# Two adaLN blocks, experts of the second: every expert on every row, or each row in blocks of its two experts

## Chip, cores and metric

One Trainium2 chip, one core. The metric is the device time of one launch in microseconds (us), the median of the runs shown. The engines are called TensorE (PE in the rows, PEld for its weight loads), VectorE (DVE), ScalarE (ACT), GpSimd (POOL) and SyncE (SP). SP, ACT and POOL can issue transfers by DMA.

## What is computed

Two transformer blocks with modulation from a condition, on 32 sequences of 256 rows of 128 numbers, all float32. Block 0 has attention with one head and a feed-forward part whose inputs are quantised to FP4 in groups of 16. Block 1 has causal attention with 16 heads and a mixture of 4 usable experts (8 are given, 4 reserved), of which each row takes the two with the largest weight:

```
logits = xf @ gate_w.T
logits = where(expert_ids >= E - N_RESERVED, -inf, logits)
top_w, top_idx = top_k(softmax(logits), 2)
top_w = top_w / sum(top_w)
cw = zeros((T, E)).at[arange(T)[:, None], top_idx].add(top_w)
h = silu(einsum('td,edh->teh', xf, w1)) * einsum('td,edh->teh', xf, w3)
y = einsum('teh,ehd->ted', h, w2)
out = einsum('te,ted->td', cw, y)
...
x = x + gb * out
```

d is 128, h is 704 (five chunks of 128 and a tail of 64). Routing depends on the data.

## The kernel before

**Pairs and turns.** Two sequences (512 rows, four tiles of 128) make a pair; there are 16. The program is a software pipeline: one turn of it holds work on up to five pairs. `sp_order`, `pool_order`, `act_order`, `dve_order` and `pe_order` (L98 to L163) are lists written out by a planner: `do(3, "turn2")` means the step turn2 on the pair that is three ahead of the turn's own. `turns` (L440) runs a list for the turns -4 to 15; turns 1 to 11 are a hardware loop. Each engine goes through its list in order, and a step waits on semaphores for what it reads. Leads 4 and 3 are block 0 (normalise, attention, quantise, feed forward), leads 3 to 1 block 1's attention and routing, leads 1 and 0 the experts. `USES` (L71) says which of seven PSUM banks a step uses, in the order in which the banks pass from one to the next; the eighth bank is `y_ps`.

**The experts before.** All weights stay in SBUF: `wg_hi`, `wg_lo`, `wu_hi`, `wu_lo` (each a float32r half of the gate or up weights) and `wd`. The 4 x 704 columns are 22 chunks. For each chunk `gate` (L1517) and `up` (L1525) call `product` (L1488): three float32r matmuls of 128 x 128 weights with all 512 rows of the pair (high with high, low with high, high with low). ACT takes tanh of the gate bank (L828), DVE makes two passes of 512 elements (`swish` L1197, `times` L1205), and `down` (L1501) adds the chunk into `y_ps` with float32 matmuls, one for each tile (each is recorded as two). After an expert's last chunk DVE's `mix` (L1183) adds `y_ps`, times the expert's weight for each row, into `mixed`; `finish` (L1207) multiplies by the gate row and adds the residual, and ACT stores the pair (L832). Every row passes all four experts; for two of them its weight is zero. `route` (L1155) on DVE finds these weights from eight small operations.

**GpSimd and SyncE before.** In a turn POOL does four times two operations on 128 x 4 numbers (`root`, L626: a power, then a product). SP issues all loads and the reorderings of q, k, v through DRAM, some 40 transfers in a turn.

## Time and profile before

| what | value |
|---|---|
| runs | 1847.67, 1849.63, 1865.75 us |
| median | 1849.63 us |
| span of the profiled execution | 1859.1 us |
| PE, PEld busy | 1694.8, 1331.0 us |
| DVE, ACT, POOL busy | 1612.1, 828.0, 82.2 us |
| mean DMA rate | 53 GB/s |

The span runs from the first to the last instruction of one profiled execution. No time of its own is given for that execution beside its span; the span stands 9.5 us above the median of the runs. Busy times of matmuls are modelled, and those of matmuls that overlap are counted once in a group, but twice in the sum of two groups: the spacing of starts is the safer measure.

### The profile page before, as it was taken

To read this page: it belongs to the slowest core of one execution; us is meant where nothing else is said; L and a number is where in the kernel's file an instruction comes from. 1 tells how busy PE (TensorE), PEld (TensorE's weight loads), DVE (VectorE), ACT (ScalarE), POOL (GpSimd) and SP (SyncE) were. 2 spreads that over 40 slices of the span, in tenths; PEclk is the share of its full clock that TensorE was granted. 3 is DMA by queue.
4 is the path that set the end of the run, shared out by engine and by line. 5 is a ranking of instruction groups with operands and counts; after the bars stand their busy time and mean duration, and the time that the engine had idled before them with its cause. 6 is when DMAs were issued, how large, how long until landed. Compare 5 with 4: busy or idle time off the path is not lost.

```text
span 1859.1 us, 37192 instructions
## 1 busy us (share of the span) xinstructions
PE 1694.8 (91%) x12297; PEld 1331.0 (72%) x12297; DVE 1612.1 (87%) x3572; ACT 828.0 (45%) x1705; POOL 82.2 (4%) x142
## 2 busy tenths in 40 slices
PE   3457799999999999999999999999999999999998
PEld 2235577777877777787776778777777878777787
DVE  5767898998899899999899899989989999897775
ACT  2234454362635436363544526354452636444431
POOL 1000101000000100000010000001000000000000
PEclk9766898999999999999999999999999999999999
DMA  5030304021030302103040300304030030303000
GB/s 163 9 105 2 111 2 114 8 76 46 18 105 4 114 9 76 46 18 102 4 120 4 107 16 18 103 4 120 4 109 15 18 103 3 111 3 103 2 18 6
DMA packets 130178, 98.50 MB, mean 53 GB/s; under 512 B 28000, under 2 KB 124512, under 8 KB 125824
## 3 DMA queue, kind: packets, MB, share of 16 engines
q1 hardware_dynamic: 115344, 86.87, 16.3%
q10 hardware_dynamic: 14640, 9.06, 1.7%
q8 instruction: 119, 1.95, 0.5%
q14 instruction: 75, 0.61, 0.1%
HBM read 56.48 MB, written 29.98 MB: 47 GB/s over the span
## 4 chain that ended last, share of the span: by engine, by line
PE 73%; DVE 15%; issue 5%; ACT 4%; ACTq 1%; SPq 1%; POOL 0%; DMA 0%; DVEq 0%; POOLq 0%
PE y_ps L1497 16%; PE bank L1490 8%; PE bank L1492 7%; PE bank L1491 7%; DVE mneg L1111 6%; PE bank L1248 5%; PE bank L1394 4%; PE bank L1457 4%; PE bank L1364 2%; PE bank L1438 2%; PE bank L1348 2%; PE bank L1390 2%; PE bank L1441 2%; PE bank L1343 2%; PE bank L1375 2%
## 5 line engine op out<-in xcount | busy, mean ns | idle before, releaser
L1497 PEld LDWEIGHTS y_ps<-wd,h 128*128 128x128 f32 (+1 forms) x3072 | 379.9, 191 | 60.3 <-issue 33.3
L1497 PE MATMUL y_ps<-wd,h 128*128 128x128 f32 (+1 forms) x3072 | 413.2, 281 | 0.7 <-DVE mixed L1190 0.5
L828 ACT ACTIVATE tt<-bank 128x512 f32<-128x512 f32 x352 | 210.9, 599 | 434.1 <-PE bank L1492 350.0
L1197 DVE SCALAR_TENSOR_TENSOR tt<-tt,bank 128x512 f32<-128x512 f32 x352 | 238.2, 683 | 30.0 <-ACT tt L828 23.3
L1205 DVE TENSOR_TENSOR h<-tt,bank 128x512 f32<-128x512 f32 x352 | 235.4, 681 | 17.4 <-PE bank L1492 7.4
L1111 DVE TENSOR_REDUCE mneg<-bank 128x2 f32<-128x512 f32 (+1 forms) x384 | 236.6, 682 | 1.7 <-PE bank L1394 1.5
L785 ACT ACTIVATE arena<-bank 128x512 f32<-128x512 f32 x384 | 198.1, 604 | 25.1 <-PE bank L1438 15.5
L1490 PE MATMUL bank<-h_hi,wu_hi 128*128 128x512 f32 x352 | 169.8, 482 | 16.9 <-DVE tt L1197 14.0
L1490 PE MATMUL bank<-h_hi,wg_hi 128*128 128x512 f32 x352 | 159.7, 454 | 3.7 <-DVE tt L1197 3.7
L1119 DVE TENSOR_TENSOR arena<-arena,keep_k 128x1024 f32<-128x1024 f32 (+1 forms) x96 | 149.0, 1577 | 13.0 <-ACT arena L785 11.6
L1492 PE MATMUL bank<-h_lo,wu_hi 128*128 128x512 f32 x352 | 141.5, 402 | 0.0
L1491 PE MATMUL bank<-h_hi,wu_lo 128*128 128x512 f32 x352 | 141.0, 401 | 0.0
L1491 PE MATMUL bank<-h_hi,wg_lo 128*128 128x512 f32 x352 | 140.9, 400 | 0.0
L1492 PE MATMUL bank<-h_lo,wg_hi 128*128 128x512 f32 x352 | 140.4, 399 | 0.0
L628 POOL TENSOR_TENSOR rstd_a<-ve_a,mhalf 128x4 f32<-128x4 f32 x48 | 48.4, 1009 | 1595.1 <-DVE ve_a L990 1595.1
L1248 PE MATMUL bank<-ident,xh 128*128 128x128 f32 x256 | 43.2, 295 | 72.3 <-ACT xh L837 33.3
L1248 PE MATMUL bank<-ident,arena 128*128 128x128 f32 (+1 forms) x640 | 91.7, 286 | 19.0 <-DVE arena L909 9.1
L1490 PEld LDWEIGHTS bank<-h_hi,wu_hi 128*128 128x128 f32 x352 | 67.1, 190 | 54.6 <-DVE tt L1197 15.7
L1248 PEld LDWEIGHTS bank<-ident,arena 128*128 128x128 f32 (+1 forms) x640 | 72.7, 144 | 34.7 <-DVE arena L909 9.7
L1390 PE MATMUL bank<-mask_q,ident_b 128*128 128x256 bf16 (+1 forms) x384 | 87.1, 320 | 11.0 <-DVE mneg L1111 10.8
L1248 PEld LDWEIGHTS bank<-ident,xh 128*128 128x128 f32 x256 | 30.7, 148 | 87.1 <-issue 30.5
L1457 PE MATMUL bank<-arena,vals 128*32 128x256 f32 x1024 | 89.2, 403 | 2.7 <-DVE arena L1119 2.5
(189 smaller groups left out, 2803.8 us busy)
## 6 DMA issues: line engine op xcount, KB each, us to landing
q_stack<-q_rows SPq DMA_DIRECT2D x16, 1024.0 KB, 4.9
k_stack<-k_rows SPq DMA_DIRECT2D x16, 1024.0 KB, 7.3
q_rows<-qk_halves SPq DMA_DIRECT2D x48, 256.0 KB, 2.8
k_rows<-qk_halves SPq DMA_DIRECT2D x48, 256.0 KB, 4.0
rows<-mod_rows SPq DMA_DIRECT2D x48, 128.0 KB, 3.8
rows<-mod_rows SPq DMA_DIRECT2D x16, 384.0 KB, 3.8
x_in<-in_L_attn_X SPq DMA_DIRECT2D x16, 256.0 KB, 4.0
vals<-arena SPq DMA_DIRECT2D x128, 32.0 KB, 2.5
```

Of the source, the lines that this page charges most:

```text
L785: frees(a(prob(u, g), ps.bank(use)[:], ACT.Exp, scale=SCALE1), use)
L828: send(a(tt[:, ch % 2, :], ps.bank(f"eg{ch}")[:], ACT.Tanh, scale=0.5), tanh_ready)
L1111: frees(v.tensor_reduce(dst, ps.bank(use)[:].rearrange("p (h k) -> p h k", k=P if name[0] == "A" else S), AX, ALU.max, negate=True), use)
L1119: send(v.tensor_tensor(x, x, keep_k[:].unsqueeze(1).to_broadcast([P, GROUPS * 512 // n, P]), ALU.min), covered)
L1197: frees(v.scalar_tensor_tensor(tt[:, ch % 2, :], tt[:, ch % 2, :], 1.0, ps.bank(f"eg{ch}")[:], ALU.add, ALU.mult), f"eg{ch}")
L1205: frees(v.tensor_tensor(h32[:, ch % 3], tt[:, ch % 2, :], ps.bank(f"eu{ch}")[:], ALU.mult), f"eu{ch}")
L1248: return nc.tensor.transpose(dst, src, ident[at:at + n, at:at + n])
L1457: mm(dst[32 * g:32 * g + 32, c:c + S], vals[:, :, 2 * h], prob(ue, g)[:, S * i:S * (i + 1)], start=True, stop=False, skip_group_check=True)
L1490: mm(dst, w_hi, h4_hi[:], start=True, stop=False)
L1491: mm(dst, w_lo, h4_hi[:], start=False, stop=False)
L1492: return mm(dst, w_hi, h4_lo[:], start=False, stop=True)
L1497: ins = mm(y_ps[:, P * t:P * (t + 1)], h32[rows_, ch % 3, P * t:P * (t + 1)], wd[rows_, ch, :], start=first and t == 0, stop=last_ and t = ...
```

## The change

**Rows go to queues.** For each pair POOL works out the two experts of every row (`route`), PE counts by matmuls how many earlier rows chose the same expert (`ranks_in`), and POOL writes, with eight indirect DMAs of 128 rows, each row twice into a queue in DRAM, once per expert (`scatter`). A queue row has 272 numbers: the normalised and modulated row, the gate row times the expert's share (128), the row's number, padding.

**Experts work on blocks.** The expert work of a turn is a group of four blocks of 256 rows of one expert. POOL's `make_table` picks the blocks (an expert's next 256 rows, while it has so many) in 26 operations on one partition. There are 17 groups: 16 of four blocks, and one of three blocks with what is left. A block has three units of two chunks (704 is filled up to 768), so a group has 12 units, the last 9. For a unit `gate` and `up` each do two chunks of three matmuls with 256 columns; tanh, swish and times still work on 512 elements (2 chunks x 256 rows); `down` has two matmuls for each chunk. A block is turned by PE and split by ACT and DVE first (`lift`).

**Weights stream.** At the start all expert weights are written to DRAM as 12 units of 128 x 1280 numbers (655 KB). SP loads the unit of each step into a ring of six (`weights`); the address comes from POOL's table. SP also loads the four blocks (`blocks`), 278 KB each.

**Results are added in DRAM.** SP stores the residual of a pair to `acc` (`store3`). After a block DVE multiplies `y_ps` by the gate rows (`weigh_rows`, 256 elements), and POOL adds it to `acc` with two indirect DMAs (`add_rows`), each block after the one before has landed. `mix`, `finish`, `begin` and `halves4` go; `route` leaves DVE. At the end SP copies `acc` (4.2 MB) to the output in DRAM.

**Orders.** All five lists and `USES` are new, with 12 units where 22 chunks were. A pair's rows must be queued before its group starts, and a group starts after the next pair's rows are queued, so the expert work comes one turn later: turns -4 to 17, of which 2 to 11 are the loop; turns 15, 16 and 17 hold expert work alone.

```diff
+SLOTS = 2 * P
+BLOCKS = 2 * TOK // SLOTS
+UNITS = MHP // (2 * P)
+GROUPS_MOE = PAIRS + 1
+LAST_STEPS = (EXP - 1) * UNITS
+RING = 2 * UNITS
+UNITW = 10 * P
+ROWW = 272
-FIRST, LAST = 4, 0
-LOOPS = PAIRS - 1 - FIRST - LAST
+FIRST = 4
+LOOP_AT, LOOPS = 2, 10
...
 def sp_order(do):
 
-    do(1, "stack_v"), do(1, "load3"), do(1, "stack_max"), do(1, "turn_att"), do(3, "load2"), do(0, "load4"), do(2, "store_q")
...
+    do(2, "load4"), do(2, "stack_max"), do(2, "stack_v"), do(1, "weights", 0), do(1, "weights", 1), do(1, "blocks")
+    do(1, "weights", 2), do(1, "weights", 3), do(4, "load2"), do(1, "weights", 4), do(1, "weights", 5), do(3, "store_q")
...
-    do(2, "stats3"), do(3, "stats2"), do(1, "stats4"), do(4, "stats1")
+    do(2, "stats3"), do(3, "stats2"), do(4, "stats1"), do(1, "stats4"), do(0, "add_rows", 0), do(1, "modulate4"), do(1, "route")
+    do(0, "add_rows", 1), do(1, "scatter"), do(0, "add_rows", 2), do(1, "table"), do(0, "add_rows", 3)
...
+            def blocks(it):
...
+                for b in range(BLOCKS):
...
+                    if it.earlier():
+                        sp.wait_ge(added.sem, added.at(it.earlier(), 2 * b + 2))
...
+                    at = sp.value_load(table[0:1, b:b + 1], min_val=0, max_val=QROWS - SLOTS)
+                    send(sp.dma_start(blk[:, b], queue[bass.ds(at, SLOTS), :].rearrange("(t p) d -> p t d", p=P)), blk_loaded[b])
+
+            def weights(it, u):
...
+                sp.wait_ge(table_ready.sem, table_ready.at(it, 1))
...
+                    sp.wait_ge(down_done.sem, down_done.at(old, k + 1))
...
+                src = w_all[bass.ds(e * UNITS + u % UNITS, 1)].rearrange("o p c -> (o p) c")
+                send(sp.dma_start(wring[:, u % RING, :], src), w_loaded[u % RING])
...
+            sp.wait_ge(added.sem, 16 * (2 * BLOCKS * (GROUPS_MOE - 1) + 2 * (LAST_STEPS // UNITS)))
+            for n in range(4):
+                at = NB * S // 4 * n
+                sp.dma_start(out.rearrange("b s d -> (b s) d")[at:at + NB * S // 4], acc[at:at + NB * S // 4]).then_inc(s_done, 16)
...
+            def scatter(it):
...
+                for t in range(TILES):
+                    for k in range(2):
+                        send(g.indirect_dma_start(queue, bass.IndirectOffsetOnAxis(ap=place[:, TILES * k + t:TILES * k + t + 1], axis=0),
+                                                  pay[:, t, k, :], None, bounds_check=QROWS - 1, oob_is_err=True), scattered)
...
+            def add_rows(it, b):
+
+                pool.wait_ge(y_ready.sem, y_ready.at(it, b + 1))
...
+                for t in range(2):
+                    send(g.indirect_dma_start(acc, bass.IndirectOffsetOnAxis(ap=blk[:, b, t, IDCOL:IDCOL + 1].bitcast(I32), axis=0),
+                                              ys[:, b % 2, t, :], None, bounds_check=DUMP + SLOTS - 1, oob_is_err=True,
+                                              compute_op=ALU.add), added)
...
-            def mix(it, e):
...
+            def weigh_rows(it, b):
...
+                y = y_ps[:, SLOTS * (b % 2):SLOTS * (b % 2 + 1)].rearrange("p (t d) -> p t d", d=P)
+                send(v.tensor_tensor(ys[:, b % 2], y, blk[:, b, :, P:2 * P], ALU.mult), y_ready)
...
-            def product(dst, w_hi, w_lo):
-
-                mm(dst, w_hi, h4_hi[:], start=True, stop=False)
-                mm(dst, w_lo, h4_hi[:], start=False, stop=False)
-                return mm(dst, w_hi, h4_lo[:], start=False, stop=True)
...
+            def product(dst, w_hi, w_lo, b):
+
+                for c in range(2):
+                    at = slice(SLOTS * c, SLOTS * (c + 1))
+                    w = slice(P * c, P * (c + 1))
+                    mm(dst[:, at], w_hi[:, w], xs_hi[:, b % 2, :], start=True, stop=False)
+                    mm(dst[:, at], w_lo[:, w], xs_hi[:, b % 2, :], start=False, stop=False)
+                    last = mm(dst[:, at], w_hi[:, w], xs_lo[:, b % 2, :], start=False, stop=True)
+                return last
```

**PE, in the loop.** Before, the end of one gate chunk, a step of another pair, and one `down` (`h` is h4 in the products, the expert's hidden rows in the down matmuls):

```order
L1490 MATMUL bank<-h_hi,wg_hi 128x512
L1491 MATMUL bank<-h_hi,wg_lo 128x512
L1492 MATMUL bank<-h_lo,wg_hi 128x512
L1269 REGISTER_ALU
L1303 MATMUL bank<-wv_s,arena 128x128 x4
L1508 ISA
L1497 MATMUL y_ps<-wd,h 128x128 x8
```

Now, a gate unit ahead of the same step (L1619, value0), with three `down` units around it:

```order
L1814 MATMUL bank<-xs_hi,wring 128x256
L1815 MATMUL bank<-xs_hi,wring 128x256
L1816 MATMUL bank<-xs_lo,wring 128x256
L1814 MATMUL bank<-xs_hi,wring 128x256
L1815 MATMUL bank<-xs_hi,wring 128x256
L1816 MATMUL bank<-xs_lo,wring 128x256
L1825 REGISTER_ALU
L1830 MATMUL y_ps<-wring,h 128x128 x8
L1588 REGISTER_ALU
L1619 MATMUL bank<-wv_s,arena 128x128 x4
L1830 MATMUL y_ps<-wring,h 128x128 x4
```

Three products with 512 columns became six with 256; `down` (L1497, now L1830) has four matmuls for a unit of two chunks, where each chunk had four.

**POOL, in the loop.** Before, the end of a turn, which holds four such couples in all:

```order
L628 TENSOR_TENSOR rstd_b<-ve_b,mhalf 128x4
L630 TENSOR_TENSOR shift_b<-mv_b,rstd_b 128x4
L627 REGISTER_ALU
L628 TENSOR_TENSOR rstd_a<-ve_a,mhalf 128x4
L630 TENSOR_TENSOR shift_a<-mv_a,rstd_a 128x4
```

Now, behind the same four couples, a later part of the turn: each row's place, the scatter to the queues, one block's result added, and the first of the table's 26 operations:

```order
L845 TENSOR_TENSOR place_f<-half_sum 128x8
L795 REGISTER_ALU
L881 CAST place<-place_f 128x8
L883 REGISTER_ALU
L887 DMA queue<-pay,place 34816x272 x8
L934 REGISTER_ALU
L937 REGISTER_ALU
L941 DMA acc<-ys,blk 8448x128 x2
L897 ISA
L899 REGISTER_ALU
L903 TENSOR_TENSOR scratch<-ends,taken 1x4
```

POOL has 62 operations and 16 DMAs in a turn where it had 8 operations, and the table, for which SP's loads wait, stands behind the scatter and behind a block's result.

## Rows read from the trace of the kernel before

**Rows 1.** The page: busy times, PEclk in 40 slices, the last chain by engine.

```profile
PE 1694.8 (91%) x12297; PEld 1331.0 (72%) x12297; DVE 1612.1 (87%) x3572; ACT 828.0 (45%) x1705; POOL 82.2 (4%) x142
...
PEclk9766898999999999999999999999999999999999
...
PE 73%; DVE 15%; issue 5%; ACT 4%; ACTq 1%; SPq 1%; POOL 0%; DMA 0%; DVEq 0%; POOLq 0%
```

**Rows 2.** Busy time by stretch: stretch, its length, engines (instructions), PEclk, DMA share, GB/s.

```profile
0.00:301.80 301.80, 203.75 (x1314) 147.03 (x1314) 224.15 (x537) 120.10 (x256) 20.53 (x40) 0.84 0.23 66
301.80:411.70 109.90, 107.06 (x768) 84.96 (x769) 99.19 (x221) 51.10 (x107) 4.83 (x8) 0.95 0.18 53
411.70:1491.00 1079.30, 1034.45 (x7662) 817.69 (x7661) 986.96 (x2191) 510.95 (x1060) 48.34 (x80) 0.99 0.19 53
1491.00:1859.10 368.10, 349.58 (x2557) 281.29 (x2556) 301.80 (x626) 145.83 (x283) 8.46 (x14) 0.99 0.14 41
...
100.00:200.00 100.00, 70.51 (x490) 46.96 (x489) 69.93 (x163) 41.47 (x91) 4.83 (x8) 0.74 0.19 57
```

**Rows 3.** PE in order of time, near the end: start, duration, line, operation.

```profile
1792.04 0.39 PE L1490 MATMUL bank<-h_hi,wg_hi 128*128 128x512 f32 x1
1792.27 0.39 PE L1491 MATMUL bank<-h_hi,wg_lo 128*128 128x512 f32 x1
1792.51 0.40 PE L1492 MATMUL bank<-h_lo,wg_hi 128*128 128x512 f32 x1
...
1793.53 2.95 PEld L1497 LDWEIGHTS y_ps<-wd,h 64*128 64x128 f32 x24 [0.37 <-issue]
```

**Rows 4.** Groups by line: line, engine, operation, count, then busy us, mean ns, idle before.

```profile
L1491 PEld LDWEIGHTS bank<-h_hi,wg_lo 128*128 128x128 f32 x352 | 68.0, 193 | 13.1 <-issue 0.2
...
L1197 DVE SCALAR_TENSOR_TENSOR tt<-tt,bank 128x512 f32<-128x512 f32 x352 | 238.2, 683 | 30.0 <-ACT tt L828 23.3
...
L1205 DVE TENSOR_TENSOR h<-tt,bank 128x512 f32<-128x512 f32 x352 | 235.4, 681 | 17.4 <-PE bank L1492 7.4 <-PE y_ps L1497 6.8
...
L1119 DVE TENSOR_TENSOR arena<-arena,keep_k 128x1024 f32<-128x1024 f32 (+1 forms) x96 | 149.0, 1577 | 13.0 <-ACT arena L785 11.6
L1192 DVE SCALAR_TENSOR_TENSOR mixed<-y_ps,cw,mixed 128x128 f32<-128x128 f32 x192 | 53.8, 343 | 7.1 <-PE y_ps L1497 5.5
...
L1190 DVE TENSOR_SCALAR mixed<-y_ps,cw 128x128 f32<-128x128 f32 x64 | 17.9, 343 | 0.0
...
L1211 DVE TENSOR_TENSOR mixed<-mixed,rows 128x512 f32<-128x512 f32 x16 | 11.1, 692 | 0.5
...
L908 DVE TENSOR_TENSOR arena<-arena 128x704 f32<-128x704 f32 x32 | 28.5, 892 | 1.1
...
L1164 DVE TENSOR_TENSOR xh<-xh 128x64 f32<-128x64 f32 x16 | 3.6, 225 | 0.6
```

**Rows 5.** POOL's groups by line, with shapes.

```profile
L628 POOL TENSOR_TENSOR rstd_a<-ve_a,mhalf 128x4 f32<-128x4 f32 x48 | 48.4, 1009 | 1595.1 <-DVE ve_a L990 1595.1
...
L630 POOL TENSOR_TENSOR shift_a<-mv_a,rstd_a 128x4 f32<-128x4 f32 x48 | 10.0, 209 | 3.8
...
L623 POOL MEMSET k_stack<- 128x2048 f32 x1 | 1.8, 1805 | 0.0
```

**Rows 6.** Transfers by what they move: issues, KB each, median us from issue to landing.

```profile
q_stack<-q_rows SPq DMA_DIRECT2D x16, 1024.0 KB, 4.9
k_stack<-k_rows SPq DMA_DIRECT2D x16, 1024.0 KB, 7.3
...
x_in<-in_L_attn_X SPq DMA_DIRECT2D x16, 256.0 KB, 4.0
```

**Rows 7.** SP in order of time: a load's issue by SP's sequencer; one per turn.

```profile
301.84 0.87 SPq L540 DMA_DIRECT2D x_in<-in_L_attn_X  x1
411.66 0.64 SPq L540 DMA_DIRECT2D x_in<-in_L_attn_X  x1
...
1490.97 0.67 SPq L540 DMA_DIRECT2D x_in<-in_L_attn_X  x1
```

More of the change, by code:

```diff
@@ L164, with behind, exists @@
+def behind(name):
+    return 1 if name.startswith(("eg", "eu", "X")) else 0
+def exists(name, n):
+    if not behind(name):
+        return 0 <= n < PAIRS
+    step = UNITS * int(name[1:]) if name[0] == "X" else int(name[2:])
+    return 0 <= n < GROUPS_MOE - 1 or n == GROUPS_MOE - 1 and step < LAST_STEPS
 class Turn:
@@ L238, in turned_over @@
     def turned_over(self, it, name):
         n = self.place[name]
[L243 to L244 removed]
+        lead, _, _, bank, _, _ = USES[n]
+        for back in range(1, (FIRST + 2) * len(USES)):
             turn, at = divmod(n - back, len(USES))
[L246 removed]
+            old_lead, old, _, old_bank, _, _ = USES[at]
             if old_bank != bank:
                 continue
[L249 to L251 removed]
@@ L252, in turned_over @@
-        return None
+            before = Turn(it.reg, it.plus + behind(name) - lead + turn + old_lead - behind(old))
+            if it.reg is not None or exists(old, before.plus):
+                return self.freed_at(before, old)
+        return None, it, 0
 def adaln_two_blocks(nc, X, Wq, Wk, Wv, bq, bk, bv, w_gate, w_up, w_down, c0, wmod0,
@@ L445, in do @@
                 def do(lead, name, *which):
-                    if reg is not None or 0 <= plus + lead < PAIRS:
-                        it = Turn(reg, plus + lead)
+                    moe = name in MOE
+                    n = plus + lead - moe
+                    steps = which[0] if name in ("gate", "up", "down", "swish", "times", "weights") else UNITS * which[0] if which else 0
+                    there = 0 <= n < GROUPS_MOE - 1 or n == GROUPS_MOE - 1 and steps < LAST_STEPS if moe else 0 <= n < PAIRS
+                    if reg is not None or there:
+                        it = Turn(reg, n)
                         mine[name](it, *which)
@@ L646, in _, with scatter_and_flush @@
+            def scatter_and_flush(it):
+                scatter(it)
+                if it.reg is None and it.plus == PAIRS - 1:
+                    flush()
+            turns(pool, pool_order, dict(stats1=stats1, stats2=stats2, stats3=stats3, stats4=stats4, modulate4=modulate4, route=route,
+                                         scatter=scatter_and_flush, table=make_table, add_rows=add_rows))
         @block.scalar
@@ L664, in _ @@
+            act.wait_ge(s_padt, 1)
             for e in range(EXP):
[L665 to L671 removed]
@@ L919, in _ @@
             v.memset(fp4_in[96:P, 2, :], 0.0)
+            for m in range(2):
+                v.memset(stage[m][:, :, MH:MHP], 0.0)
             v.memset(fp4_in[96:P, 5, :], 0.0).then_inc(s_zero, 1)
@@ new lines, in lift @@
+            def lift(it, b):
+                pe.wait_ge(blk_loaded[b].sem, blk_loaded[b].at(it, 1))
+                free(it, f"X{b}")
+                for t in range(2):
+                    last = turn(ps.bank(f"X{b}")[:, P * t:P * (t + 1)], blk[:, b, t, 0:P])
+                send(last, ps.signal_ready(f"X{b}"))
+            def product(dst, w_hi, w_lo, b):
[6 more added lines that the diff above has]
+                return last
@@ new lines, in down @@
+            def down(it, u):
+                b, j, n = u // UNITS, u % UNITS, u % RING
+                evacuated(it, f"eu{u}")
+                if j == 0:
+                    old, k = previous(it, b, 1, BLOCKS)
+                    if old:
+                        pe.wait_ge(y_ready.sem, y_ready.at(old, k + 1))
+                for c in range(2):
+                    rows_ = slice(0, TAIL) if j == UNITS - 1 and c == 1 else slice(0, P)
+                    for t in range(2):
+                        at = SLOTS * (b % 2) + P * t
+                        last = mm(y_ps[:, at:at + P], h32[rows_, u % 3, SLOTS * c + P * t:SLOTS * c + P * (t + 1)], wd[rows_, n, P * c:P * (c + 1)],
+                                  start=j == 0 and c == 0 and t == 0, stop=j == UNITS - 1 and c == 1, skip_group_check=True)
+                send(last, down_done)
```

751 lines of the change are left out of this document (469 added, 282 removed), and 52 rows, old and new, of the table USES.

## The prediction

> **What bounds the kernel now.** I read the page first: PE is busy 91% of the span, DVE 87%, POOL 4%, and the last chain runs through PE for 73% and DVE for 15% [rows 1]. The start is not the rule, so next comes a turn in the loop. SP's x_in load marks turns: from 411.66 to 1490.97 us there are ten, 107.9 us each [rows 7]. In that stretch PE is busy 1034.5 us, 103.4 a turn, DVE 987.0, 98.7 a turn, POOL 4.8 a turn, and the clock is 0.99 [rows 2]. So PE bounds, DVE is 5 us behind it, and a turn lasts 4.5 us more than PE's work. A cut in PE's work alone would end at DVE after 5 us; the change cuts both.
>
> Then PE in order of time, for the price of expert work. Products with 512 columns start 0.23 us apart (0.233 over the three rows), and 24 down records take 2.95 us, 0.123 each [rows 3]. I don't take the groups' busy times for these, since their 0.4 us overlap.
>
> **Expert work, before, per turn.** PE: 22 chunks x 6 products x 0.233 = 30.8 us, and 96 down matmuls (22 x 4, and two tails of 4 more) x 2 records x 0.126 (between 0.123 and what a turn shows) = 24.2; together 55.0. DVE [rows 4]: swish 238.2 and times 235.4 over 16 turns are 29.6; mix (53.8 + 17.9) / 16 = 4.5; finish, begin and h4's low half, four passes at 0.4 to 0.7, 2.5; route about eight at 0.22, 1.7. Together 38.3.
>
> **Expert work, after, per full turn.** 12 units where 22 chunks were, because a row meets two experts, not four, and a unit holds as much as a chunk (2 x 256 for 512), less the padding to 768.
> - Products: 12 x 12 = 144 with 256 columns. No row shows this shape at 128 rows. Half of 0.233 is 0.117; the other end is a weight load of 0.193 (L1491, [rows 4]), should it be no longer hidden. But in rows 3 a load of the same width comes every 0.123 us without holding the down matmuls, so I take 0.127: 18.3 us (bounds 16.8 and 27.8).
> - Down: 48 matmuls, 96 records x 0.126 = 12.1. Lifting four blocks, eight transposes, and the rank matmuls: 1.7. PE: 32.1, 22.9 less; 80.5 a turn.
> - DVE: 12 x 1.346 = 16.2; four lifts and four weigh_rows of 256 elements, each between the 128-element row 0.343 and the 512-element row 0.68, 0.46: 3.7. Together 19.8, 18.5 less; 80.2 a turn.
>
> PE and DVE now have the same 80 us, so neither covers the other's waits; I add 7.5, not 4.5: 88 us a turn (bounds 85 and 97). That is 19.9 less.
>
> **What hides beside it.** POOL: four couples as now, 4 x 1.22 = 4.9; 53 small operations at 0.21 plus 0.08 for the step's own semaphore, about 15, one of them a power at 1.0; five of 512 elements, each between 0.45 (a quarter of the 1.8 us memset of 2048) and 1.8, taken at 1.4, twice DVE's 0.69: 7 [rows 4, 5]. Then 16 indirect DMAs. The trace has no DMA on POOL. The lower bound is SP's issue, 0.65 [rows 7], the upper one a whole transfer, 4.0 [rows 6]; I take 1.6, the issue plus one slow POOL operation (1.01), since addresses are made by software there. Sum 27 + 16 x 1.6 = 53 us of 88: hidden, as long as nothing waits for its end. What waits: after ranks_in, at 56% of PE's list, come scatter (8), add_rows (2), the table (26 x 0.28 = 7.3 us) and add_rows (2), for which 37 us are left; it takes 8 + 12 x 1.6 = 27. So the limit is 2.4 us per DMA.
>
> One rule speaks to this price: the Trainium skill, "DMA: Bandwidth & Descriptors", section "Anatomy of one DMA — SWDGE (gpsimd) path", puts about 2.0 us fixed on such a DMA, most of it the receipt and little the making of descriptors. By it POOL would be held less than I take and the sum would stay; no run here shows it yet.
>
> DMA: 655 KB for each unit. Two stacks of 1024 KB land in 7.3 us, one in 4.9 [rows 6], so 2.3 to 3.2 us each if nothing is in the way, 28 to 38 a turn; what runs now is 0.19 of 108, 20 us [rows 2]. Some 60 us of 88, and the ring is half a turn ahead. Hidden. The waits of `blocks` for the last addition hold up behind them weights 2 to 5 and load2 on SP; half a turn covers that, except at the end.
>
> POOL and DVE side by side: nothing in rows 2 shows a price, as POOL works 4.8 us a turn. Bounds 0 and 6.5 us a turn; taken 0.7, 12 us in all.
>
> **The other turns.** Turn 0 has no expert work now: 109.9 us [rows 2] become about 85, -25. Turn -1 loses seven chunks, but weights are split, written to DRAM and read back: 0 net (-7 to +15). Turns 12 to 15 took 368.1 us with 349.6 of PE [rows 2]. Less 4 x 55.0 and with 3 x 32.1, turns 12 to 14 have 225.9 of PE; at 88 / 80.5 that is 247. Turns 15 to 17, 33 units alone: PE 32.1 + 32.1 + 24.1 = 88. Here nothing covers the way from down 8 over weigh_rows (0.5), an addition (3.2), the table (7.3), the last addition (3.2 + 4.0) and SP's loads (1.3 + 4.0), 24 us, beside five units' 13: twice 11. With 0.6 us of bare waiting per unit: 130. The end: last addition 7, and 4.2 MB from DRAM to DRAM; 2 MB in 7.3 us makes 15, twice that if reading and writing share; taken 23: 30. Together 407, +39.
>
> **Sum**, against the profiled span: 1859.1 - 11 x 19.9 (219) - 25 + 0 + 12 + 39 = 1666 us. The span stands 0.5% above the median of the runs; the same for the changed kernel gives 1658.
>
> **Rivals.**
> 1. *POOL's queue bounds; slower.* One mechanism: an indirect DMA holds POOL longer than 2.4 us, the table comes late, SP's loads and the next turn's first lift wait. Each us above 2.4 adds 12 us a turn, over some 14 turns. From 3.6 us (102 a turn) the kernel is no faster than before; at 4.0, the upper bound, a turn is 107 and the run about 1925. For it: nothing in the trace prices 128 addresses made by software, and an idle POOL (4%) proves nothing about a full one. Against: even its power takes only 1.01.
> 2. *The shared port.* DVE passes with both inputs in SBUF (cover 149.0 / 16 = 9.3 us a turn; L908 and its three like at 28.5 / 16 = 1.8 each, 7.1; a few more, some 20 together [rows 4]) stop POOL's reads and are stopped by them. A quarter of POOL's 27 us then costs DVE up to 6.5 us a turn: 94, in all 1658 + 80 = 1738. The Trainium skill, "SBUF — State Buffer", section "Who interferes with whom", has this rule: a DVE instruction with two SBUF inputs contends with a GpSimd instruction that reads SBUF. Rows 2 neither bear it out nor speak against it.
> 3. *Weight loads bound the short products.* At 0.193 each PE has 90.0 a turn, and the turn is 94.5: about 1748. Against it rows 3, for it that an f32r product may need more than a float32 pass.
> 4. *The way through DRAM.* Ranks, scatter, table, weights, blocks, lift is a loop over turns; where transfers queue behind 655 KB loads, each leg is 3 to 5 us longer, and a turn 97: about 1784. The 10 us that 37 - 27 leave speak against it.
>
> That the change doesn't do what it says can hardly be: the counts of units are fixed in the lists.
>
> **Chances.** Forecast, 1600 to 1720: 0.52. Rival 1: 0.17, of which 0.15 slower. Rival 2: 0.12. Rival 3: 0.08. Rival 4: 0.11, of which 0.03 near no change. A measurement of this kernel tells about 1% from no change; so faster by over 1%: 0.52 + 0.12 + 0.08 + 0.08 = 0.80, within 1%: 0.05, slower: 0.15. The range runs from 1590 (turns of 85, a cheap end) to 1800 (rival 4), which leaves out rival 1 and little else. The likeliest case by itself holds 1600 to 1720.
>
> Not in the sum is PE's clock in the last three turns: with PE busy 70.5 of 100 us in the start's second stretch the granted clock was 0.74 [rows 2], and 88 us at 0.75 would be 29 more. The range holds it.
>
> **What would show it.** Right: ten turns between x_in loads at 86 to 91 us each, PE and DVE both busy 79 to 83 in them; products 0.12 to 0.13 us apart; POOL busy 45 to 60 a turn, its DMAs 1 to 2 us apart; POOL's waits for DVE and for y_ready, none of PE for the ring. Turns 15 to 17 and the end: some 160 us. Wrong: a turn over 95 us; PE's lift or SP's loads waiting for the table; DVE passes of cover (L1119) longer than 1.58 us on the mean; POOL's DMAs 3 us apart; products 0.19 apart; or the final copy over 35 us.

## The result, and the profile after

The changed kernel takes 1944.51 us in the median (1938.76 to 1951.63, 4 runs), the kernel before 1855.89 (1847.67 to 1865.75, 4 runs) beside it: ratio 1.0482, 95% interval 1.0437 to 1.0528. The forecast was 1658, range 1590 to 1800. The profiled execution took 1939.09 us, its span 1937.2.

The page of the changed kernel (as rows 1): busy times, PEclk, the last chain by engine.

```profile
PE 1483.3 (77%) x11345; PEld 1181.7 (61%) x11345; DVE 1407.3 (73%) x2951; ACT 750.0 (39%) x1627; POOL 806.3 (42%) x1324
...
PEclk9777686998798978999897998798978879795887
...
PE 38%; DVE 19%; issue 10%; POOL 5%; SPq 4%; DMA 3%; ACT 3%; DVEq 1%; another core or an unknown queue 0%; POOLq 0%; ACTq 0%
```

PE lost 211 us of work, DVE 205, and the kernel got longer: no engine is near its bound any more, and PEclk, 9 nearly throughout in rows 1, moves between 7 and 9 in the loop.

SP's x_in loads (as rows 7), then busy time by stretch (as rows 2): turn 0, nine turns of the loop, from turn 11's load to the end.

```profile
284.37 1.50 SPq L638 DMA_DIRECT2D x_in<-in_L_attn_X  x1
367.30 0.57 SPq L638 DMA_DIRECT2D x_in<-in_L_attn_X  x1
472.03 0.38 SPq L638 DMA_DIRECT2D x_in<-in_L_attn_X  x1
...
1408.00 0.38 SPq L638 DMA_DIRECT2D x_in<-in_L_attn_X  x1
```

```profile
284.37:367.30 82.93, 64.04 (x461) 42.51 (x462) 66.55 (x149) 38.92 (x88) 38.73 (x70) 0.73 0.46 146
472.03:1408.00 935.97, 795.18 (x6258) 643.08 (x6257) 769.22 (x1604) 411.12 (x900) 444.09 (x702) 0.89 0.52 158
1408.00:1937.00 529.00, 365.67 (x2854) 314.70 (x2854) 285.65 (x544) 148.63 (x302) 229.94 (x383) 0.82 0.53 160
```

Ten turns (1 to 10) last 104.1 us each, where 88 were forecast and 107.9 were before. In nine of them PE is busy 88.4 us a turn, DVE 85.5, POOL 49.3, at a mean clock of 0.89. The loads measure turns, but they don't compare the start and the end of the two kernels: x_in was last but one in SP's list and is second now, so it stands elsewhere against PE's work. The matmuls of `logits` stand for the same rows in both. Pair 1's and pair 12's, on PE in order of time, before and now:

```profile
306.31 1.70 PE L1484 MATMUL bank<-gw_s,h 128*128 128x4 f32 x8
1494.03 0.95 PE L1484 MATMUL bank<-gw_s,h 128*128 128x4 f32 x8
```

```profile
303.80 1.84 PE L1786 MATMUL bank<-gw_s,h 128*128 128x4 f32 x8 [1.26 <-ACT h L1149]
1435.40 1.87 PE L1786 MATMUL bank<-gw_s,h 128*128 128x4 f32 x8 [4.62 <-DVE h L1526]
```

The start, up to pair 1's logits, went from 306.3 to 303.8 us; the eleven turns from there from 1187.7 to 1131.6; the rest of the span from 365.1 to 501.8. The forecast's terms for these three are -25, -219 with +12 for the port, and +39. So 22 us were lost at the start, 151 in the turns and 98 at the end. Some 16 of these 98 belong to the turns (an estimate: half a group's PE work of 32.1 us now comes behind pair 12's logits and not ahead of them), which makes it about 167 and 82.

What PE waited for in those nine turns: what, on what, us in total, times, longest.

```profile
PE bank L1786 <- DVE h L1526: 41.6, 9, 4.6
PE bank L1743 <- DMA q_stack<-arena: 36.0, 9, 4.0
PE bank L1569 <- DVE arena L1473: 24.3, 18, 2.4
```

Three waits stand out in every turn: 4.6 us in front of `logits` for VectorE, 4.0 in front of `rows` 0 for SP's eight small loads of `stack_max`, and two that together make 2.7 for VectorE's `turn_out`. The first, on DVE and POOL in order of time (a fence for each):

```profile
1011.96 2.97 DVE L1244 TENSOR_TENSOR arena<-arena,qiv 128x704 f32<-128x704 f32 x1
1014.96 1.47 DVE L1246 TENSOR_SCALAR arena<-arena 128x704 int32<-128x704 int32 x1
1016.46 1.47 DVE L1247 TENSOR_SCALAR arena<-arena 128x704 f32<-128x704 f32 x1
1018.14 0.69 DVE L1526 TENSOR_TENSOR h<-tt,bank 128x512 f32<-128x512 f32 x1 [0.21 <-DVE arena L1247]
...
1058.83 0.89 DVE L1244 TENSOR_TENSOR arena<-arena,qiv 128x704 f32<-128x704 f32 x1
1059.75 0.53 DVE L1246 TENSOR_SCALAR arena<-arena 128x704 int32<-128x704 int32 x1
```

```profile
1012.33 1.84 POOL L828 TENSOR_TENSOR pay<-xh,rows 128x512 f32<-128x512 f32 x1
1014.24 1.80 POOL L831 TENSOR_TENSOR pay<-pay,rows 128x512 f32<-128x512 f32 x1
1016.01 1.54 POOL L832 TENSOR_TENSOR pay<-pay,rows 128x512 f32<-128x512 f32 x1
```

While POOL makes the three passes of `modulate4`, three quantise passes on DVE take 5.9 us; the same three take 1.95 us where POOL has small work. PE's next matmul waits for what stands behind them. What the stall does to the clock shows in windows of 3 us (columns as in rows 2):

```profile
1012.50:1015.50 3.00, 1.84 (x17) 1.65 (x15) 2.97 (x2) 1.27 (x3) 2.92 (x3) 1.00 0.72 147
1015.50:1018.50 3.00, 0.00 (x0) 0.00 (x0) 2.76 (x3) 0.00 (x0) 2.35 (x3) 0.64 0.63 207
1018.50:1021.50 3.00, 2.54 (x12) 2.55 (x13) 1.92 (x7) 0.01 (x1) 0.00 (x0) 0.50 0.00 0
1021.50:1024.50 3.00, 3.00 (x19) 1.52 (x19) 1.77 (x3) 0.80 (x2) 1.91 (x6) 0.50 0.00 0
...
1030.50:1033.50 3.00, 3.00 (x19) 2.71 (x18) 1.31 (x4) 0.60 (x2) 1.54 (x2) 0.52 0.41 119
1033.50:1036.50 3.00, 2.82 (x25) 1.86 (x22) 2.19 (x5) 1.48 (x4) 2.55 (x3) 1.00 0.97 330
```

PE stands, the clock goes to 0.50, the lower of its two levels (1.2 GHz), and stays there for some 14 us in which PE is busy. PE in order of time shows the price: products of 256 columns start 0.21 us apart there, 0.12 at the upper level.

```profile
1021.47 0.41 PE L1814 MATMUL bank<-xs_hi,wring 128*128 128x256 f32 x1
1021.68 0.41 PE L1815 MATMUL bank<-xs_hi,wring 128*128 128x256 f32 x1
...
1053.68 0.28 PE L1816 MATMUL bank<-xs_lo,wring 128*128 128x256 f32 x1
1053.80 0.28 PE L1814 MATMUL bank<-xs_hi,wring 128*128 128x256 f32 x1
```

POOL's indirect DMAs and the widest DVE pass by group (as rows 4):

```profile
L941 POOL DMA_INDIRECT acc<-ys,blk x134 | 228.0, 1702 | 244.4 <-DVE ys L1514 181.8
...
L887 POOL DMA_INDIRECT queue<-pay,place x128 | 136.7, 1068 | 49.7 <-issue 35.2
L1466 DVE TENSOR_TENSOR arena<-arena,keep_k 128x1024 f32<-128x1024 f32 (+1 forms) x96 | 151.5, 1578 | 37.4 <-ACT arena L1128 37.2
```

And PE's wait for blocks after 1700 us, 71 us in three waits: the last groups.

```profile
PE bank L1569 <- DMA blk<-queue: 71.0, 3, 39.3
```

### The profile page after: what moved, and what is told of

The parts are those of the page before. It is cut to its first block, busy times and chain, and to the rows that moved or that the text cites. A ratio compares the mean times of both kernels' runs of the same rounds, so it can differ in the third digit from the quotient of the medians.

```text
span 1937.2 us, 38860 instructions
## 1 busy us (share of the span) xinstructions
PE 1483.3 (77%) x11345; PEld 1181.7 (61%) x11345; DVE 1407.3 (73%) x2951; ACT 750.0 (39%) x1627; POOL 806.3 (42%) x1324
## 4 chain that ended last, share of the span: by engine, by line
PE 38%; DVE 19%; issue 10%; POOL 5%; SPq 4%; DMA 3%; ACT 3%; DVEq 1%; another core or an unknown queue 0%; POOLq 0%; ACTq 0%
PE y_ps L1830 8%; PE bank L1701 3%; PE bank L1814 3%; SPq L735 3%; PE bank L1697 3%; PE bank L1569 3%; PE bank L1815 2%; PE bank L1816 2%; DVE arena L1244 2%; DVE mneg L1458 2%; PE bank L1672 2%; PE bank L1625 2%; PE bank L1762 2%; PE bank L1743 2%; PE bank L1746 1%
## 5 line engine op out<-in xcount | busy, mean ns | idle before, releaser
L941 POOL DMA_INDIRECT acc<-ys,blk x134 | 228.0, 1702 | 244.4 <-DVE ys L1514 181.8
L1814 PE MATMUL bank<-xs_hi,wring 128*128 128x256 f32 x804 | 291.1, 362 | 21.7 <-issue 7.1
L1176 ACT ACTIVATE tt<-bank 128x512 f32<-128x512 f32 x201 | 118.1, 595 | 395.1 <-PE bank L1816 317.2
L1830 PE MATMUL y_ps<-wring,h 128*128 128x128 f32 (+1 forms) x1608 | 260.1, 311 | 12.2 <-DVE h L1526 12.2
L1830 PEld LDWEIGHTS y_ps<-wring,h 128*128 128x128 f32 (+1 forms) x1608 | 232.1, 216 | 37.2 <-issue 17.7
L1815 PE MATMUL bank<-xs_hi,wring 128*128 128x256 f32 x804 | 245.6, 305 | 0.0
L1816 PE MATMUL bank<-xs_lo,wring 128*128 128x256 f32 x804 | 243.7, 303 | 0.0
L1814 PEld LDWEIGHTS bank<-xs_hi,wring 128*128 128x128 f32 x804 | 173.6, 216 | 52.2 <-issue 32.7
L1526 DVE TENSOR_TENSOR h<-tt,bank 128x512 f32<-128x512 f32 x201 | 137.0, 685 | 81.2 <-PE bank L1816 60.8
L1815 PEld LDWEIGHTS bank<-xs_hi,wring 128*128 128x128 f32 x804 | 173.6, 216 | 10.0 <-issue 7.4
L1518 DVE SCALAR_TENSOR_TENSOR tt<-tt,bank 128x512 f32<-128x512 f32 x201 | 135.6, 683 | 59.3 <-ACT tt L1176 57.6
L1466 DVE TENSOR_TENSOR arena<-arena,keep_k 128x1024 f32<-128x1024 f32 (+1 forms) x96 | 151.5, 1578 | 37.4 <-ACT arena L1128 37.2
L1816 PEld LDWEIGHTS bank<-xs_lo,wring 128*128 128x128 f32 x804 | 172.3, 214 | 0.0
L887 POOL DMA_INDIRECT queue<-pay,place x128 | 136.7, 1068 | 49.7 <-issue 35.2
L1569 PE MATMUL bank<-ident,arena 128*128 128x128 f32 (+1 forms) x640 | 96.6, 289 | 38.8 <-DVE arena L1473 33.2
L1569 PE MATMUL bank<-ident,xh 128*128 128x128 f32 x256 | 46.2, 310 | 79.2 <-ACT xh L1181 34.7
L1569 PEld LDWEIGHTS bank<-ident,arena 128*128 128x128 f32 (+1 forms) x640 | 75.0, 146 | 51.9 <-DVE arena L1473 36.6
```

The lines of the kernel that those rows point to most:

```text
L887: send(g.indirect_dma_start(queue, bass.IndirectOffsetOnAxis(ap=place[:, TILES * k + t:TILES * k + t + 1], axis=0), pay[:, t, k, :], None, ...
L941: send(g.indirect_dma_start(acc, bass.IndirectOffsetOnAxis(ap=blk[:, b, t, IDCOL:IDCOL + 1].bitcast(I32), axis=0), ys[:, b % 2, t, :], Non ...
L1466: send(v.tensor_tensor(x, x, keep_k[:].unsqueeze(1).to_broadcast([P, GROUPS * 512 // n, P]), ALU.min), covered)
L1526: frees(v.tensor_tensor(h32[:, u % 3], tt[:, u % 2, :], ps.bank(f"eu{u}")[:], ALU.mult), f"eu{u}")
L1569: return nc.tensor.transpose(dst, src, ident[at:at + n, at:at + n])
L1814: mm(dst[:, at], w_hi[:, w], xs_hi[:, b % 2, :], start=True, stop=False)
```

## The experiments

Theory, from here on: each stall of PE costs its length and then a stretch at half the clock; one of the stalls comes from the port that DVE and POOL share. All of the first seven and the eleventh are edits to the changed kernel. Ratios are to the kernel before, which ran beside each. Runs one to four ran on one chip, five to seven on a second, eight to eleven on a third, the twelfth on a fourth.

**First: modulate4 behind the ranks.**

```diff
-    do(0, "add_rows", 0), do(1, "modulate4"), do(1, "route")
+    do(0, "add_rows", 0), do(1, "route")
...
             def route(it):
...
+                modulate4(it)
                 gate_row = rows4[:, :, 2 * P:3 * P].unsqueeze(2).to_broadcast([P, 2, 2, P])
```

> Edit: GpSimd's three passes of 512 elements of modulate4 come after the ranks of route, no longer before them. Nothing is left out. In the changed kernel these passes run at the same time as VectorE's quantise passes of 704 elements (L1244, L1246, L1247), which then take 2.97, 1.47 and 1.47 us where the same passes elsewhere take 0.89, 0.53 and 0.53; TensorE stands for 5 us behind them and shows half the clock for up to 13 us after. Theory P (the two engines collide, and the stall brings the clock down): the three passes go back to some 2.0 us together, DVE's busy time falls 4 us a turn, the stall shrinks under 2 us, the mean granted clock in the loop rises from 0.89 to 0.93 or more, a turn goes from 104 to 96 to 100 us, the kernel from 1944 to 1840 (1810 to 1880). Rival Q (GpSimd's 5 us of passes cost VectorE the same wherever they lie, since VectorE is busy 82% of the time with such passes): another VectorE pass gets longer by as much, and the turn stays within 1.5 us of 104.

1912.15 us, ratio 1.0317 (1.0244 to 1.0391). DVE falls to 81.4 us a turn, as expected of the collision, but the turn only to 102.5. A new stall shows in the waits of ACT and DVE, with a releaser that the profile does not know:

```profile
ACT arena L1119 <- remote: 94.7, 9, 12.9
DVE h L1527 <- remote: 80.7, 11, 8.4
```

In one turn of the first run ACT's step L1119, whose matmuls end on PE at 1039.6 us, starts at 1046.5, while POOL issues ten indirect DMAs from 1034.9 to 1048.8:

```profile
1038.53 1.08 PE L1729 MATMUL bank<-mneg,ident 128*16 128x64 f32 x16
1046.45 0.59 ACT L1119 ACTIVATE arena<-bank 16x512 fp32r<-16x512 f32 x1 [10.89 <-remote]
```

Theory P's mechanism stands; part of its price was given back in this new stall, which the twelfth run takes up.

**Second: rows 0 behind scores0 0 and down 9.**

```diff
-    do(2, "rows", 0), do(4, "scores0", 0), do(0, "down", 9), do(0, "up", 11)
+    do(4, "scores0", 0), do(0, "down", 9), do(2, "rows", 0), do(0, "up", 11)
```

> Edit: in TensorE's order the step rows 0 of the pair two ahead, which waits for the eight small loads of stack_max, comes behind scores0 0 and down 9. Nothing is left out. In the changed kernel TensorE stands 4.0 us a turn there, and what follows shows half the clock for some 6 us. Theory S (a stall of the order costs its own length and a stretch at half the clock): TensorE's wait for q_stack falls from 4.5 us a turn to 1.5 or less, a turn from 104 to 99 or 101, the kernel to 1890 (1870 to 1915). Rival V (VectorE sets the turn: it is busy 85.5 of 104 us and works through this stall): the wait at q_stack goes, TensorE waits as long somewhere later in the turn, the turn stays within 1 us of 104 and the kernel within 15 us of 1944.

1952.86 us, ratio 1.0563 (1.0515 to 1.0611). The wait for q_stack falls from 4.0 to 1.7 us a turn, a new one of 1.7 us (a product, for ACT) appears, and the turn is 105.6. Moving a wait by a few steps gains nothing: rival V as to the time.

**Third: the table right behind scatter.**

```diff
-    do(1, "scatter"), do(0, "add_rows", 2), do(1, "table"), do(0, "add_rows", 3)
+    do(1, "scatter"), do(1, "table"), do(0, "add_rows", 2), do(0, "add_rows", 3)
```

> Edit: in GpSimd's order the table comes right behind scatter, before the addition of block 2. Nothing is left out. Theory T (in the last three turns the way down, weigh_rows, addition, table, addition, loads is walked with nothing beside it, 54.2 us a turn from one load of blocks to the next at 1774.3, 1828.5 and 1882.8): these fall to 44 or 48 us each, the loop stays within 1 us of 104, and the kernel gains 15 to 35 us: 1920. Rival R (the loop too waits for the table, so that SP's loads come late in every turn): turns of 101 or less and a kernel below 1900. Rival N (the last additions' landing, 6 us, is what the loads wait for anyway): turns at the end stay over 51 us, and the kernel within 10 us of 1944.

1944.62 us, ratio 1.0517 (1.0459 to 1.0575). Turn 104.4; the loads of the last groups are 54 us apart as before. Rival N: the loads wait for the last addition anyway.

**Fourth: a thin weight stream.**

```diff
-                send(sp.dma_start(wring[:, u % RING, :], src), w_loaded[u % RING])
+                w = UNITW if first_pair(it) else 8
+                send(sp.dma_start(wring[:, u % RING, 0:w], src[:, 0:w]), w_loaded[u % RING])
```

> Edit: from the second group on a unit's weight load brings 8 of 1280 columns; the experts then work with weights left in the ring. Left out: nearly all of the weight stream (some 122 of 129 MB). Every wait and every issue stays. Theory D0 (the stream is hidden in the loop): a turn stays within 1.5 us of 104, and only the last three turns gain, 2 or 3 us each where a load's landing lies on the path; kernel 1925 to 1944. Rival D (the 655 KB loads hold up the small loads behind them: stack_max, blocks, the q and k rows): the stall at q_stack shrinks by over 1 us, a turn goes to 100 or less, the kernel below 1890.

1944.13 us, ratio 1.0519 (1.0453 to 1.0585). With half the bytes gone (DMA share 0.52 to 0.31) the turn is 106.0; only the last groups come 48 us apart, not 54. In the loop the stream is hidden.

**Fifth: the quantise passes behind logits.**

```diff
-    do(0, "swish", 4), do(3, "quantise_h", 0, 0), do(0, "times", 3), do(3, "quantise_h", 0, 1), do(0, "times", 4)
-    do(3, "gate0", 2), do(0, "swish", 5), do(1, "logits"), do(3, "up0", 2), do(0, "times", 5), do(0, "swish", 6)
+    do(0, "swish", 4), do(0, "times", 3), do(0, "times", 4), do(3, "gate0", 2), do(0, "swish", 5), do(1, "logits")
+    do(3, "quantise_h", 0, 0), do(3, "up0", 2), do(0, "times", 5), do(3, "quantise_h", 0, 1), do(0, "swish", 6)
```

> Edit: the order of GpSimd is the changed kernel's; in VectorE's order the first two parts of quantise_h of half 0 (one maximum, then the passes L1244, L1246, L1247 that met GpSimd's modulate4) come behind times 3, times 4, swish 5 and logits. Nothing is left out. The first run moved GpSimd's passes instead: DVE's busy time fell from 85.5 to 81.4 us a turn as theory P has it, but the turn only from 104.1 to 102.5, since ACT and DVE then stood up to 12.9 and 8.4 us in every turn for signals of TensorE while GpSimd issued ten indirect DMAs in a row. Theory P with theory W (each collision is worth its stall; the second loss comes from where that row of DMAs falls, not from the repair): here the row of DMAs stays where it was, the three passes take 2.0 us or up to 3 beside GpSimd's small operations, TensorE's wait in front of logits falls from 4.6 to under 1 us, a turn to 96 to 99 us, the kernel to 1870 (1840 to 1895). Rival Q2 (the turn is held at 102 or more by something that neither repair touches): turn 101 to 104, kernel 1905 to 1945.

1902.75 us, ratio 1.026 (1.0185 to 1.0335); turn 100.5, DVE 82.3 us of it. The passes are short again:

```profile
904.07 0.89 DVE L1244 TENSOR_TENSOR arena<-arena,qiv 128x704 f32<-128x704 f32 x1
904.99 0.59 DVE L1246 TENSOR_SCALAR arena<-arena 128x704 int32<-128x704 int32 x1
905.61 0.53 DVE L1247 TENSOR_SCALAR arena<-arena 128x704 f32<-128x704 f32 x1
```

The collision is worth 3.6 us a turn, less than expected: PE's wait in front of logits is gone, but 3.7 us of it come back in front of `maxima` 1, with half the clock behind it (mean still 0.89).

**Sixth: more work for PE, where it waits.**

```diff
+            def filler(dst, n):
+                for _ in range(n):
+                    mm(dst[:].rearrange("p (n k) -> p n k", k=P), ones_b[:], before_b[:].unsqueeze(1).to_broadcast([P, 4, P]),
+                       start=True, stop=True, skip_group_check=True)
...
             def up(it, u):
...
                 free(it, f"eu{u}", needs=(f"X{u // UNITS}",))
+                if u == 5:
+                    filler(ps.bank("eu5"), 18)
```

In gate 1 there are 9 in the same place, in rows 0 there are 14 between the wait for the banks and that for q_stack.

> Edit: TensorE gets more work: 41 bf16 matmuls of 512 columns a turn, which write only banks that the next matmul overwrites, put ahead of its three waits (9 ahead of gate 1, 18 ahead of up 5, 14 ahead of rows 0), about 9 us at the full clock. Nothing is left out. Theory C (TensorE's clock falls after each stall and what that costs is a good part of the turn): the stretches at half the clock disappear or halve, the mean granted clock in the loop goes from 0.89 to 0.95 or more, and the turn falls in spite of the added work, from 104 to 96 to 100 us; kernel 1890 (1850 to 1915). Rival L (the clock does not matter, the waits on VectorE do): the clock rises but the turn stays at 103 to 105. Rival A (added work adds): a turn of 107 or more, kernel over 1975.

1878.06 us, ratio 1.0137 (1.0058 to 1.0215), 66 us faster than the changed kernel with 9 us more work on PE in each turn. Nine turns of the loop:

```profile
466.92:1345.32 878.40, 814.65 (x6631) 626.77 (x6629) 768.81 (x1604) 411.08 (x900) 449.10 (x702) 0.99 0.55 169
```

The clock is 0.99, the turn 97.7. PE is busy 90.5 us; less the added 9 (an estimate: 41 at the 0.22 us from start to start), its own work is 81.5, where it took 88.4 at 0.89.

POOL's order shows something else here: in all ten turns of this run the eight DMAs of scatter and the two of the next addition follow each other at once, as in the first run, and no wait of ACT or DVE has an unknown releaser. ACT's same step starts 0.04 us after its matmuls:

```profile
999.67 1.05 POOL L887 DMA_INDIRECT queue<-pay,place  x1 [0.98 <-POOL place L881]
...
1010.66 1.60 POOL L941 DMA_INDIRECT acc<-ys,blk  x1 [0.30 <-issue]
1012.57 1.56 POOL L941 DMA_INDIRECT acc<-ys,blk  x1 [0.30 <-issue]
```

```profile
1009.44 1.08 PE L1728 MATMUL bank<-mneg,ident 128*16 128x64 f32 x16
1010.56 0.59 ACT L1118 ACTIVATE arena<-bank 16x512 fp32r<-16x512 f32 x1 [4.09 <-PE bank L1728]
```

**Eleventh, its control: the same 41 matmuls where PE has no wait,** ahead of rows 3.

> Edit to the changed kernel: the same 41 extra matmuls of 512 columns a turn as in the sixth run, all at one place, ahead of rows 3, where TensorE has no wait and shows the full clock. Nothing is left out. Theory C (the extra work helps only where it keeps TensorE busy through a wait): the three waits and the half clock behind them stay, and the 9 us add: turn 110 to 114, kernel 2010 to 2060. Rival O (any extra work shifts the order or raises the clock as a whole): turn 104 or less.

2135.8 us, ratio 1.1493 (1.1417 to 1.157); turn 118.1. Added work adds, and more than its 9 us: the waits stay (4.6 and 4.2 us), a new one of 4.5 us a turn appears (L1569, no releaser known), and the clock is 0.86.

**Seventh: blocks one by one among the weight loads** (with the third run's table).

```diff
-    do(1, "weights", 1), do(1, "blocks"), do(1, "weights", 2), do(1, "weights", 3), do(4, "load2"), do(1, "weights", 4), do(1, "weights", 5)
+    do(1, "weights", 1), do(1, "blocks", 0), do(1, "blocks", 1), do(1, "weights", 2), do(1, "weights", 3), do(4, "load2")
+    do(1, "blocks", 2), do(1, "weights", 4), do(1, "weights", 5), do(1, "blocks", 3)
```

> Edit: the table comes right behind scatter as in the third run, and SP's step blocks is cut into four that stand between the weight loads (blocks 0 and 1 behind weights 1, blocks 2 behind load2, blocks 3 behind weights 5). Nothing is left out. In the changed kernel each of the last turns is 54.2 us from load to load of blocks; the third run showed that an earlier table alone leaves this at 54.2, since block 3's load waits for the landing of the last addition and weights 2 to 5 stand behind it. Theory T2 (that order of SP is what makes the last turns serial): a turn at the end falls to 38 to 46 us, the kernel gains 25 to 45 us: 1910; the loop stays within 1 us of 104. Rival N2 (the last turns are bound by the chain of units itself: products, tanh, two passes, down at half the clock): over 50 us a turn at the end, kernel within 12 us of 1944.

1919.62 us, ratio 1.0336 (1.0261 to 1.0411). The last groups come 47 us apart, the loop stays (105.3). PE still stands 36.6 us once: POOL's way for the last pair, in order of time: eight DMAs of scatter from 1744.61 on, eight of flush from 1756.43 on, then the table until 1776:

```profile
1744.61 1.06 POOL L887 DMA_INDIRECT queue<-pay,place  x1 [0.95 <-POOL place L881]
...
1756.43 1.03 POOL L955 DMA_INDIRECT queue<-padt,pad_place  x1 [0.81 <-POOL pad_place L950]
...
1766.49 0.19 POOL L903 TENSOR_TENSOR scratch<-ends,taken 1x4 f32<-1x4 f32 x1
```

**Eighth, ninth, tenth: the parts together.** The eighth has the fifth's order, the seventh's loads, `flush` behind the last full table, and the extra matmuls at the three waits that are then left; the ninth adds matmuls ahead of the last groups' lifts; the tenth is the eighth with the collision put back.

> Edits together: VectorE's order of the fifth run; the table behind scatter and the four blocks of the seventh; the padding of the queues (flush, eight indirect DMAs, 11.7 us on GpSimd at 1755 to 1767 in the seventh run, where TensorE stands for 37 us) behind the last full table; and TensorE's extra matmuls of the sixth run, with those of the middle place moved: 9 ahead of gate 1, 16 in front of maxima 1 (where TensorE stood 3.7 us in the fifth run), 14 ahead of rows 0, none in gate 1 from group 14 on. Nothing is left out. If the parts add up (theory C for the clock, P for the collision, T2 for the end): turn 97.7 less 2 or 3 for VectorE's 4 us: 94 to 96; from the last x_in load to the end 529 (sixth run) less 30 to 40; kernel 1810 (1790 to 1840), below the kernel before. Rival X (VectorE's 81 us and its waits hold the turn at 97 once the clock is full, so that the repair of the collision is worth nothing more): turn 97 to 98, kernel 1835 to 1860.

> The eighth kernel, and 90, 40 and 40 extra matmuls of 512 columns ahead of the first lift of groups 14, 15 and 16, where TensorE stands for some 25, 12 and 12 us. Nothing is left out. Theory C at the end: the units of the last three groups run at the full clock, a group of 12 units gets 3 to 5 us shorter, the kernel 8 to 15 us faster than the eighth. Rival U (the units of the last groups are bound by their chain over tanh and two VectorE passes, not by TensorE): within 4 us of the eighth.

> The eighth kernel with VectorE's order of the changed kernel and the 18 extra matmuls back ahead of up 5: the collision on the shared port stays (passes of 2.97, 1.47 and 1.47 us). Nothing is left out. Theory P beside a full clock: the turn is that of the sixth run, 97 to 98, and the kernel 25 to 40 us slower than the eighth, 1840. Rival X: the same as the eighth within 8 us.

Eighth: 1842.43 us (10 runs), ratio 0.9928 (0.9896 to 0.996), the first that beats the kernel before, by 0.7%. Ninth: 1840.03, ratio 0.9921 (0.9892 to 0.9951), the same within the intervals, though the extra matmuls filled PE's waits for blocks at the end (44.8 us before, 9.4 now) and raised the clock of the last 136 us from 0.83 to 0.88: rival U. Tenth: 1866.85, ratio 1.0054 (1.0025 to 1.0083). The loop of the eighth and of the tenth:

```profile
471.85:1340.17 868.32, 815.77 (x6635) 627.56 (x6627) 740.75 (x1604) 411.75 (x903) 439.52 (x702) 0.98 0.55 171
```

```profile
467.29:1355.06 887.77, 819.69 (x6600) 625.07 (x6599) 766.81 (x1599) 411.11 (x897) 439.27 (x702) 0.97 0.54 167
```

With a full clock the collision is worth 2.3 us a turn and 24 us in all (1866.85 against 1842.43); some 0.4 of the 2.3 are the two more extra matmuls of the tenth. The parts add up less well than expected (1810): a turn is 96.4, not 95, and the end from turn 11's load is 503 us, 26 less than in the sixth run, where 30 to 40 were expected.

**Twelfth: the first run's kernel with pauses between the DMAs of scatter.**

```diff
                                                   pay[:, t, k, :], None, bounds_check=QROWS - 1, oob_is_err=True), scattered)
+                        step(g.tensor_tensor(norm[:], norm[:], minus1[:], ALU.pow))
```

> Edit: the first run's kernel (modulate4 behind the ranks), with a power of 128 x 4 numbers, about 1.0 us, and its wait behind each of the eight indirect DMAs of scatter, so that their starts lie 2.5 us apart, not 1.29. Nothing is left out. In the first run's kernel ACT and VectorE wait up to 12.9 and 8.4 us in every turn for signals of TensorE, with a releaser that the profile does not know, while ten indirect DMAs follow each other at once. Theory W (a row of indirect DMAs without a pause holds back signals to the other engines): the waits with the unknown releaser, 231 us over the first run's kernel, fall under 60, and the turn from 102.5 to under 100 although GpSimd works 10 us more a turn. Rival V2 (it is the number of indirect DMAs or their transfers, not the lack of a pause, or GpSimd's place in the turn): the waits stay over 150 us in sum, and the turn at 102 or more.

2082.72 us, ratio 1.1227 (1.1171 to 1.1283). No wait of ACT or DVE with an unknown releaser is left (231 us before), but this doesn't show theory W: the sixth run has the same row of ten without a pause and no such wait either. Such waits occur in the changed kernel (41 us in sum) and in runs one to four (231, 40, 69 and 60 us), of which only the first has ten DMAs in a row; in runs five to twelve, on other chips, there are none. So the cause of the first run's new stall is not shown. The turn, moreover, went to 112.7: POOL now needs 58 us a turn, the chain that sets a turn goes through scatter, table, additions and SP's loads, and PE stands 13.5 us a turn for the normalised rows of ACT at its end. That is close to the forecast's rival 1, made by hand: it sets in between 49 and 58 us of POOL a turn.

## Why the prediction was wrong

**What held.** PE's own work: 80.5 forecast, 81.5 at the full clock (sixth run). DVE: 80.2 forecast, 81.4 without the collision (first run). Short products: 0.127 forecast, 0.12 measured, so rival 3 is out. POOL: 53 forecast, 49.3 measured; indirect DMAs at 1.07 and 1.70 us for 1.6. On their price the Trainium skill, "DMA: Bandwidth & Descriptors", section "Anatomy of one DMA — SWDGE (gpsimd) path", had said that little of the fixed 2.0 us is the making of descriptors; POOL was in fact held for over 1 us by each, and here the measurement decides. Since that is under 2.4 us, rival 1 did not hold in the loop, nor did rival 4: the weight stream and the loads are hidden (fourth run).

**Where the loop's 16 us a turn come from.** The step that failed is "so neither covers the other's waits; I add 7.5": what had to be added to the 80.5 us of PE's work was 23.6. A turn of 104.1 is 81.5 of PE's work, 6.9 that the half clock adds to it, and 15.7 of waiting. So:
- *The clock, 6.9 us of PE's time, 6.4 of the turn by the sixth run.* It was put outside the sum for the last three turns and not thought of for the loop. The row for it was in rows 2 (PE busy 70.5 of 100 us, clock 0.74): the same holds for a loop in which PE stands 4 to 5 us at a time. The sixth and the eleventh run show it from both sides: 104.1 to 97.7 with more work in the waits, 118.1 with the same work elsewhere (4.5 of them its new wait). The Trainium skill tells this pattern in "TensorE: Matmul & The Clock Gate", section "HAM oscillation — how this bites in real kernels": a wait between pieces of work lets the clock fall, and the next piece starts cold each time. The trace agrees: 0.50 for some 14 us behind a wait of 4.6. By that rule the change spoke against itself, as it took work from PE and left the waits.
- *The waits, 8 us more than forecast.* The three waits named above. The one for q_stack is the old chain from `turn_max` over eight issues of SP (5.0 us), which the old order covered with work and the new one does not; the second run shows that reordering two steps does not mend it. In the whole of the kernel before the same wait cost 3.5 us:

```profile
PE bank L1438 <- DMA q_stack<-arena: 3.5, 2, 3.0
```

- *The port, in that sum.* Taken at 0.7 us a turn, bounds 0 to 6.5; measured 4.0 of DVE's time, and of the turn 3.6 (fifth run) or 2.3 with a full clock (eighth against tenth). The forecast spread POOL's 27 us evenly and took a tenth of the upper bound. In truth one place carries all: three passes on each side, in step in every turn, with PE waiting behind them. `cover` (L1466), the largest suspect, did not move (1578 ns for 1577 in rows 4). Rival 2's rule on DVE instructions with two SBUF inputs holds for L1244 (2.97 for 0.89 us); L1246 and L1247 with one input are held up as well (1.47 for 0.53). The Trainium skill, "SBUF — State Buffer", section "Who interferes with whom", says this of DVE's fast modes that use two ports; no view here names the mode. Rival 2 alone would have given 94, not 104.

**Where the end's 82 us come from.** The forecast for turns 15 to 17 was nearly right: 130, and 135 from the first lift of turn 15 (1779.7) to the end of the last down (1914.5). From there to the end are 22.7 us, forecast 30. What failed is turns 12 to 14, put at PE's work times 88 / 80.5: "at 88 / 80.5 that is 247". From pair 12's logits to turn 15 it took 344 us, where the forecast, with the half group more, has some 260 (an estimate). PE's work shrinks there faster than the turns do: from 1512 to 1616 us PE is busy 87 of 104 us, from there to 1702.5 it is 66 of 86, and in turn 14 PE stands 39.3 us for the last pair's way over POOL: modulate, ranks, scatter, eight DMAs of `flush` that the forecast did not list at all, the table. The forecast's "11 x 19.9" is right: of the 704 records of L1491 before, 44 for each pair, 484 lie between the two logits above, which is eleven pairs.

**Where the start's 22 us come from.** Pair 0's logits come at 220.9 us, where they came at 207.1. The splitting of the weights and their writing to DRAM were put at 0 net (-7 to +15) for this stretch, and it came out 14 us longer; which part of it made it so isn't shown. From there to pair 1's logits it is 83.0 us, where it was 99.2: 16 less, where -25 was forecast. No experiment was made on the start.

**Signs.** "A turn over 95 us" and PE's lift waiting for blocks came true; longer `cover` passes, DMAs 3 us apart and a copy over 35 us did not. No listed sign looked at PEclk in the loop, which was the one that mattered.

**Left open.** What made ACT and DVE wait for PE's signals in the first run, up to 12.9 and 8.4 us in a turn. A row of indirect DMAs without a pause is not enough, as the sixth run shows; whether it takes the chip, the order of that kernel or both can't be told, since that kernel ran on one chip only.

## What to carry to other kernels

When a change takes work from a TensorE that was busy without a break, price the waits that were hidden at their length and at the half-clock stretch behind each; a few matmuls into a bank about to be overwritten, put ahead of a wait, are a cheap test of that and, in the sixth run, worth 66 us. A port collision is priced place by place from the order, two engines' rows side by side, not as a share of all the work. And a pipeline that gets a stage more and a queue through DRAM has a longer end: walk the last item through alone.
